# Query projections of the second batch in three fp32r matmuls instead of one fp32 matmul

## The reference

```
x = x + attention(layernorm(x))        # 16 heads of 64, 4 groups of keys and values
x = x + experts(layernorm(x))          # 8 experts, the best 2 of each batch
x = x + gated_attention(layernorm(x))  # chunks of 64
x = x + gated_ffn(layernorm(x))
```

## Time and profile before

| | before |
|---|---|
| median of 3 runs (lowest to highest) | 867.8 us (863.0 to 869.72) |
| the profiled execution | 862.72 us |
| its span, first to last instruction | 860.8 us |
| mean granted TensorE clock | 0.996 of full speed |
| TensorE busy | 820.8 us (95%) |
| VectorE busy | 622.1 us (72%) |
| GpSimd busy | 569.1 us (66%) |
| ScalarE busy | 468.3 us (54%) |

### The profile page before, as it was taken

The page is one execution under the profiler, slowest core; times in us unless marked ns, Lnnn a source line. Parts: engine busy times, 40 slices in busy tenths (PEclk is TensorE's granted clock), DMA queues, the critical chain, the costliest instruction groups (busy, mean ns, idle before and its releaser), DMA issues.

```text
span 860.8 us, 13541 instructions
## 1 busy us (share of the span) xinstructions
PE 820.8 (95%) x4892; PEld 444.8 (52%) x4892; DVE 622.1 (72%) x1041; ACT 468.3 (54%) x841; POOL 569.1 (66%) x373
## 2 busy tenths in 40 slices
PE   4887999999999999989889999999999999999998
PEld 3444444454444454454444444445444455996765
DVE  5668677877778877456877778777777777668663
ACT  2666555555655665656555565455566556546421
POOL 2645788678888788825467888768888786366410
PEclk9999999999999999999999999999999999999999
DMA  6000000000000000000000000000000001200001
GB/s 174 0 2 1 1 1 2 1 1 1 1 2 1 1 2 1 1 1 0 2 1 1 1 1 1 1 2 2 1 1 1 1 1 51 53 2 0 1 1 49
DMA packets 49596, 7.98 MB, mean 9 GB/s; under 512 B 42486, under 2 KB 47994, under 8 KB 49530
## 3 DMA queue, kind: packets, MB, share of 16 engines
q1 hardware_dynamic: 48666, 6.99, 5.1%
q10 hardware_dynamic: 864, 0.13, 0.1%
HBM read 5.92 MB, written 1.05 MB: 8 GB/s over the span
## 4 chain that ended last, share of the span: by engine, by line
PE 82%; DVE 11%; ACT 3%; issue 2%; POOL 2%; DMA 1%; DVEq 0%; SPq 0%; POOLq 0%; ACTq 0%
PE psum L659 26%; PE psum L644 19%; PE psum L624 12%; PE psum L528 4%; PE psum L674 4%; DVE part L1163 4%; PE psum L687 3%; PE psum L1683 3%; PE psum L1731 2%; PE psum L1721 2%; PE psum L1742 1%; DVE q_rate L1148 1%; DVE ql L1155 1%; PE psum L606 1%; ACT space L853 1%
## 5 line engine op out<-in xcount | busy, mean ns | idle before, releaser
L502 POOL TENSOR_TENSOR space<-space 128x1024 f32<-128x1024 f32 x160 | 380.5, 2378 | 26.8 <-ACT space L895 8.4
L1163 DVE TENSOR_REDUCE part<-psum 128x2 f32<-128x1024 f32 x256 | 313.2, 1224 | 113.4 <-PE psum L624 110.7
L895 ACT ACTIVATE space<-psum 128x512 f32<-128x512 f32 x512 | 264.4, 602 | 147.7 <-PE psum L644 118.3
L659 PE MATMUL psum<-space,vb 128*64 128x512 f32 x1024 | 247.5, 605 | 0.0
L624 PE MATMUL psum<-kh,qh 64*128 64x512 f32 x512 | 127.5, 494 | 11.3 <-DVE part L1163 8.1
L507 POOL TENSOR_TENSOR space<-space 128x1024 f32<-128x1024 f32 x30 | 71.6, 2387 | 97.0 <-DVE space L1179 97.0
L624 PEld LDWEIGHTS psum<-kh,qh 64*128 64x128 f32 x512 | 47.7, 183 | 146.2 <-DVE part L1163 111.7
L659 PEld LDWEIGHTS psum<-space,vb 128*64 128x64 f32 x1024 | 62.3, 136 | 106.1 <-issue 71.0
L644 PE MATMUL psum<-qh,kh 64*128 64x512 f32 x512 | 102.5, 395 | 0.0
L644 PE MATMUL psum<-ql,kh 64*128 64x512 f32 x512 | 101.3, 390 | 0.0
L644 PE MATMUL psum<-qh,kl 64*128 64x512 f32 x512 | 101.3, 390 | 0.0
(11 more groups left out here) (216 smaller groups left out, 908.5 us busy)
## 6 DMA issues: line engine op xcount, KB each, us to landing
ql<-nmx SPq DMA_DIRECT2D x256, 0.5 KB, 2.0
wproj<-in_L_ffn_W SPq DMA_DIRECT2D x4, 256.0 KB, 3.6
out<-x SPq DMA_DIRECT2D x4, 256.0 KB, 2.1
x<-in_L_attn_x SPq DMA_DIRECT2D x2, 256.0 KB, 4.5
wproj<-in_L_attn_Wq SPq DMA_DIRECT2D x1, 512.0 KB, 6.7
x<-in_L_attn_x SPq DMA_DIRECT2D x1, 512.0 KB, 8.0
wout<-in_L_attn_Wout SPq DMA_DIRECT2D x1, 512.0 KB, 6.8
w1s<-in_L_ffn_W SPq DMA_DIRECT2D x2, 256.0 KB, 2.8
```

What stands on the lines that cost most here:

```text
L502: pool.tensor_tensor(to, pt[0] if u == 1 else to, pt[u], ALU.add)\
L659: last = pe.matmul(outp[rows(h), :], vb[:, place(m)[1], kt, :], pt[kt][:, h, :], start=(kt == 0), stop=(kt == TILES - 1))
L895: act.activation(pt[kt][:, h, :], key_scores[kt % 2][h], ACT.Exp).then_inc(exp_made, 1)
L1163: dve.tensor_reduce(to[:, half, :], scores.rearrange("p (h k) -> p h k", h=2), AX_X, ALU.max, negate=True)\
```

## The change

All query projections of batch 1 (8 tiles x 2 projections x 2 banks) are made from high and low parts; batch 0 stays as it was. Each fp32 matmul becomes three fp32r matmuls into the same bank: high rows by low weights, high rows by high weights, low rows by high weights.

```diff
+            def project_split(j, to, high, low, k):
+
+                rows, w = slice(j * P, (j + 1) * P), slice(k * 512, (k + 1) * 512)
+                pe.matmul(to, c["row_high"][0][:, rows], low[:, w], start=True, stop=False)
+                pe.matmul(to, c["row_high"][0][:, rows], high[:, w], start=False, stop=False)
+                return pe.matmul(to, c["row_low"][0][:, rows], high[:, w], start=False, stop=True)
...
             (norms)
+                if b and j == 0:
+                    pe.wait_ge(x_low_made, 1)
+                    pe.wait_ge(q_low_made, 1)
                 for k in range(2):
-                    last = project(b, j, qc_at[:, k * 512:(k + 1) * 512], Q_AT + k * 512)
+                    to = qc_at[:, k * 512:(k + 1) * 512]
+                    last = project_split(j, to, c["q_high"], c["q_low"], k) if b else project(b, j, to, Q_AT + k * 512)
...
             (folded: the same with u_high and u_low, and at tile 0 a wait for u_low_made)
```

```diff
                         keep_x(1, 0, TILES)
+                        act.activation(c["row_high"][0][:, :], banks(0, 2), ACT.Identity, bias=aln_b[:, 0:1], scale=aln_s[:, 0:1]).then_inc(x_high_made, 1)
+                    if b == 0 and ph == 4 * SLOTS + 4:
+                        act.activation(c["q_high"][:, :], wproj[:, Q_AT:Q_AT + INNER], ACT.Copy).then_inc(q_high_made, 1)
...
             high_keys(1, 1)
+            act.activation(c["u_high"][:, :], wproj[:, U_AT:U_AT + INNER], ACT.Copy).then_inc(u_high_made, 1)
             square_keys(1, 3)
```

GpSimd makes the low parts (what is left after the high part is subtracted), between its last add of batch 0 and its twins of the keys, and between the third twin and the last:

```diff
                 if b:
-                    for s in range(STEPS):
+                    pool.wait_ge(x_high_made, 1)
+                    pool.tensor_tensor(c["row_low"][0][:, :], xnt[:, 1, :], c["row_high"][0][:, :].bitcast(F32), ALU.subtract).then_inc(x_low_made, 1)
+                    pool.wait_ge(q_high_made, 1)
+                    pool.tensor_tensor(c["q_low"][:, :], wproj[:, Q_AT:Q_AT + INNER], c["q_high"][:, :].bitcast(F32), ALU.subtract).then_inc(q_low_made, 1)
+                    for s in range(STEPS - 1):
                         twin(b, s)
+                    pool.wait_ge(u_high_made, 1)
+                    pool.wait_ge(y_made, SLOTS)
+                    pool.tensor_tensor(c["u_low"][:, :], wproj[:, U_AT:U_AT + INNER], c["u_high"][:, :].bitcast(F32), ALU.subtract).then_inc(u_low_made, 1)
+                    twin(b, STEPS - 1)
                     normal(b, 0)
```

More of the change, by code:

```diff
@@ L132, in build @@
         first = first_layer(nc, a, xv, x, ident, wt, psum, sb, sem, shared)
+        with ExitStack() as between:
+            shared["q_high"] = sb("q_high", [P, INNER], F32R, between)
+            shared["q_low"] = sb("q_low", [P, INNER], F32R, between)
+            shared["u_high"] = sb("u_high", [P, INNER], F32R, between)
+            shared["u_low"] = sb("u_low", [P, INNER], F32R, between)
         second = rest(nc, a, x, ident, wt, psum, sb, sem, out, shared, turn)
@@ L297, in first_layer @@
         rows0_kept = sem("rows0_kept")
+        x_high_made = sem("x_high_made")
+        x_low_made = sem("x_low_made")
+        q_high_made = sem("q_high_made")
+        q_low_made = sem("q_low_made")
+        u_high_made = sem("u_high_made")
+        u_low_made = sem("u_low_made")
         rows0_summed = sem("rows0_summed")
@@ L588, in folded @@
                     pe.wait_ge(w_folded, 1)
+                if b and j == 0:
+                    pe.wait_ge(u_low_made, 1)
                 for k in range(2):
-                    last = project(b, j, u_at[:, k * 512:(k + 1) * 512], U_AT + k * 512)
+                    to = u_at[:, k * 512:(k + 1) * 512]
+                    last = project_split(j, to, c["u_high"], c["u_low"], k) if b else project(b, j, to, U_AT + k * 512)
                 last.then_inc(u_projected, 1)
@@ L784, in tensor_part @@
             pe.wait_ge(xnt_made, 3)
+            pe.wait_ge(x_high_made, 1)
             keys_values(1, 0)
```

## The result

The changed kernel took 859.07 us in the median of 12 runs (858.39 to 864.3), the kernel before 865.77 us in 12 runs beside it (862.45 to 869.72). The medians are 6.7 us apart. The ratio measured over the runs is 0.9941, 95% interval 0.9923 to 0.9959: 5.1 us less, 3.5 to 6.7. A second set of 12 runs of the same kernel gave 0.9967 (0.9947 to 0.9987), 2.9 us less. Both are less than 1%, on the side that was forecast. The forecast was 2.3 us. The median of 859.07 lies just under the low end of the range, 859.5; the forecast started from a median of 867.8 in three runs, though, and by the ratio that becomes 862.7.

What follows compares the result with a forecast made beforehand. TensorE held 82% of the chain of waits, but VectorE and ScalarE stood between the edited projections. Terms +0.2, -0.9 and -1.6 made -2.3 us: median 867.8 becomes 865.5, shaded to 865.0, range 859.5 to 868.8.

Steps and rivals of the forecast that it cites:

- Weight loads are hidden; that rival: Rival: weight loads stand beside the split projections' matmuls, pairs cost 2.5 us, +9 to +12 us, median 878; chance 0.02.
- Tiles 0 to 3: Batch 1's projections and transposes ahead of its production loop, 386 to 403.5 us: first score pair earlier, -0.9 us.
- (a): ScalarE's added pass making high rows in the first batch's phase 65, 1.1 to 1.25 us long: +0.2 us, bounds 0 and 0.6.
- The loop: Batch 1's production loop, tiles 4 to 7: turns fall from 5.91 to 5.5 us, four turns together -1.6 us.
- the ring: One loop turn's chain: norms' projection, ScalarE square, VectorE sum and maximum, score pair; 5.91 us becomes 5.4.
- TensorE's other half: TensorE's loop work from odd score pair through transposes and folded projection; next even pair at +5.58 us, later than 5.4.
- (b) to (e): Added high weights on ScalarE, low rows and low weights on GpSimd (2.4 us each), in idle or covered time: nothing.
- the rival that needed over 2.9: Rival: GpSimd's fp32r subtractions are slow, over 2.9 us holding tile 0's folded projection; +2.1 us, median 869.9; chance 0.06.
- The sum: Whole kernel: 0.2 - 0.9 - 1.6 = -2.3 us, bounds -1.2 and -3.6.
- Absorbed: Rival: the loop's ring over three engines and a later VectorE wait eat the gain; -0.5 us, median 867.3; chance 0.20.
- More than forecast: Rival: ring free of the odd pair's lateness, 1.5 us gained before the loop; -4 us, median 863.8; chance 0.10.
- Nothing later is bound to a fixed time, so it should reach the end: Everything behind the edited part: the whole -2.3 us carries through, profiled execution 862.72 us becomes 860.4.

Runs made afterwards that it cites:

- splits-only kernel: Changed kernel with all splits and waits made but batch 1's projections kept fp32: 864.16 us, ratio 0.9993 to the kernel before.
- norms by one matmul: Changed kernel with batch 1's norms' projections as one fp32r matmul a bank, low parts left out of the sums of squares; timed: 861.89 us, ratio 0.9959.

## Why the prediction was right or wrong

- *The price of the three matmuls* was right: 0.23 us a step, 0.33 behind an fp32 block. Weight loads are hidden; that rival is out.
- *Tiles 0 to 3* were put at -0.9 and are -1.2 (to the first score pair, with (a) in it). The second group of transposes came at 400.34, 3.71 us behind the first (396.63) instead of 4.37: 0.66 us won there, where I had 0.44 (3.93); the rest was as worked out.
- *The loop* was put at -1.6 and is -1.33. The mechanism was right in the main: the ring decides three turns of the four, TensorE's own work the other. The term that was mis-sized is the start of the norms' projection behind a score pair: I took 0.34 us for the pair, it is 0.43, and the first matmul takes 0.33 and not 0.23. From the start of the pair to the end of the projection that is 416.26 - 414.17 = 2.09 us, not 1.88; so a turn by the ring is 5.59 us and not 5.4. TensorE's other half, which I had as the later one at 5.58, is early by 0.28 us at 419.76 and is the later one only in the turn that ends at 414.17.
- *(a)* was put at +0.2 and is +0.03: ScalarE starts the next instruction 0.14 us ahead of the recorded end of the one before (L982 at 356.22, L851 to 356.36), so L936 ended at 357.94 and TensorE's values started 6.98 us into the stretch instead of 6.95.
- *(b) to (e)* were put at nothing, and the splits-only kernel shows nothing. GpSimd's 2.37 us lie on the row I had taken; the rival that needed over 2.9 is out.
- *The sum* of -2.3 is near the 2.53 us of the stretch with some luck: tiles 0 to 3 were 0.3 too small, the loop 0.3 too large and (a) 0.2 too large. The bounds I gave don't follow from their own terms: with the tiles at 0.9, a loop at 0.25 a turn and 0.5 for (a) make -1.4, not -1.2, and 0.55 a turn with 1.2 before it make -3.4, not -3.6. The range of 859.5 to 868.8 was built with 3.2 and 0.9, which are neither.
- *Absorbed* is out: the 2.5 us of the stretch are all there at the start of the feed-forward matmuls (375.71 us behind the transposes of batch 1's rows before, 373.16 after).
- *More than forecast* is the nearest rival by the measured time, but not by its reason: it had the gain in the loop and ahead of it, and the stretch fell by 2.53 us, not 4.
- *"Nothing later is bound to a fixed time, so it should reach the end"* is the step that failed: it put the granted clock at nothing. The ratio has 5.1 us (2.9 in the second set), so the 2.5 us reached the end and something was added to them: the clock, by the average over all runs (2.5 us without the lost clock, 2.1 from it), most likely because the last layer, moved to an earlier time, more often met one dip instead of two. The rows could have shown it: the page's row of clocks rounds it away, but the mean of 0.996 is 3.4 us of an 861 us span. Shown: the dips, what they take from the clock, one case where a dip cost 0.5 us and not 1.71, and that two dips in the last layer return when it is put back by work (12 runs and one trace, on another chip). Not shown: what decides where they fall, and so why the earlier time had fewer. Moving by time alone can't be all of it, since blocks that started at 804.1 and 807.9 us met a dip, and one that started at 805.5 did not.

## What to carry to other kernels

Find the ring of waits that closes one turn of a loop, and count a cheaper operation in full only if it is a link of it: from three matmuls to one, the same cut was worth 1.8 us in the norms and 0.2 us beside them. Outside the loop look again, block by block: the folded projections, nearly worthless in the loop (0.2 us), won 0.8 us ahead of it. Before forecasting a change of less than 1%, turn the mean granted clock into microseconds and see where it is lost: here a dip of 1.7 us more or less is two thirds of the edit, it moves when the code in front of it moves, and a denser version can lose there all it has won. Compare such versions by a stretch of the trace, or by the time less the lost clock averaged over many runs, and not by medians alone. One trace less its dips is not enough, since a dip may fall where TensorE would have waited anyway.

## What the runs showed of the hardware

- The granted clock falls to half for 3.4 us at a time (in four traces once for twice that, at 28 us), 1.71 us lost each 3.4. Over all profiled runs the dips lie in three places: the first 60 us, the production loop and what follows it (407 to 446 us), and the last layer (797 to 827 us), where TensorE was busy throughout in the windows shown above. It needn't be: in the 3 us ahead of the dip at 432 us in the norms by one matmul it was busy for 1.54. In three runs a further one is cut off by the end of the span.
- What a dip costs in time: 1.72 us in the last layer between before and after, some 0.5 us behind the loop, nothing at the very end.
- GpSimd's subtraction of 128x1024 with fp32r output: 2.36 to 2.37 us, as its f32 add. ScalarE's fp32r copy of 128x1024 from SBUF: 1.05 to 1.08 us, and 1.24 us from PSUM with scale and bias, where the f32 pass took 1.23.
- Six fp32r matmuls of 512 columns in two banks take 1.4 us in a row (the steps from 398.95 to 400.34 us in the changed kernel), 1.61 us behind a score pair that uses half of the rows. Their six weight loads of 0.19 us each are in that time.
